# Issuing the adjacency strips of a graph kernel from two engines' DMA queues

## The chip, the cores and the metric

One core of one Trainium2 chip runs the whole program. The metric is the device time of one execution in microseconds; the median of the runs shown is what counts. A profiled execution gives the rows below.

## The reference

Two graph layers over 4096 nodes with 256 features, and a 0/1 adjacency matrix `adj` of 4096 x 4096 in float32. Cut to what matters:

```python
deg = max((adj != 0).sum(-1), 1)
pooled = (dinv * (adj + I) * dinv) @ x + x             # dinv = rsqrt(deg)
x = layernorm(x + relu(pooled @ W0 + b0))              # first layer
# second layer: h = x @ W_sa ; scores_ij = h_i.a_left + h_j.a_right
e = where(adj != 0, exp(-leaky_relu(scores, 0.01)), 0)
x_a = (e / (e.sum(1) + 1e-5)) @ h                      # attention branch
x_b = adj @ (x @ W_gcnb) + b_gcnb                      # plain branch
x = layernorm(x + sigmoid(gate_a * x_a + gate_b * x_b))
```

The gates are sigmoids of `adj @ x` and `x` projected to one column each. The adjacency is read from HBM once as float32 (64 MB) and turned into one-byte codes; both layers multiply with the codes.

## The kernel before

**Layer one, TensorE.** The rows of the output are 32 tiles of 128 (`T`), four of them to a quarter (`PT`). `sum_rows` (L1372) multiplies the codes of one quarter with `y` = x W0, split into a high and a low half-precision part, over all 32 column blocks. The first quarter is interleaved with the making of `y` (`xt_step` L1340, `z_step` L1355). From tile 4 on, `sum_tile` puts between the four parts of a tile a transpose of an earlier tile's normalised rows (`t_step`, L1392) and a projection with the weights of layer two (`p_step`, L1407). Each of these waits for other engines: `t_step(n)` for VectorE's `normalize`, `p_step(n)` for VectorE's `x1t_lo(n)` (L954) and `h_lo(n-1)` (L941).

**The adjacency.** It comes in 128 strips (`NSTRIP`) of 512 KB: strip `s` holds two column blocks (`SJ`) of quarter `s // 16`. They go into a ring of six buffers (`RING`), each with a semaphore `strip_in` of its own. A cast turns a strip into codes: ScalarE (`cast`, L513) casts the odd strips and all of strips 26 to 31, VectorE (L796) the other even ones; `on_act(s)` says which. `casts_until(s)` gives how many casts each of the two has made once strip `s` is done. The codes live in three slots, one for each quarter.

**SyncE's queue.** One loop over `s` issues all strips in order (L344). From strip 6 on it waits first for the cast of strip `s - 6`, which frees the buffer, whichever engine makes it (L340 to L342). At eight places (`CODES_AT`: after strips 32, 43, 53, 69, 85, ...) the same queue sends one quarter's codes to HBM for layer two: two DMAs of 1 MB (L332). The weights are loaded behind strip 4.

**ScalarE's order**, written out by hand: in the first 60 us, a copy `xt_copy`, one or two `y_hi` and a cast per step or two; then `cast(7)`, `x1t_copy(0)`, `cast(2)`, `x1t_copy(1)`, `proj_copies(0)`, `cast(1)`, `x1t_copy(2)`, `proj_copies(1)`, `forms_hi(0)`, `cast(1)`, `x1t_copy(3)`, `proj_copies(2)`, `proj_copies(3)`, `cast(3)`; then for each tile `proj_copies(n-3)`, `x1t_copy(n-2)`, in every second tile `forms_hi`, and `cast(2)`. `x1t_copy` (L553) also issues a DMA of 128 KB (L555), `proj_copies` begins with a wait and a DMA of 136 KB (L562), copies the projection out of the accumulator (L568 to L582) and so releases VectorE's `h_lo`. **VectorE's order** per tile: `degree`, `h_lo`, `residual`, `x1t_lo`, `stats`, `forms_lo` in every second tile, one cast, `normalize`, one cast.

Layer two (from about 320 us) reads the codes back from HBM and has no strips.

Of the kernel before, what the change touches and what calls it, by code (L numbers as in the profile page):

```python
# [19 lines left out]
PW = 256  # L20
# [3 lines left out]
SJ = 2  # L24
GS = T // SJ
NSTRIP = NQ * GS
RING = 6
# [65 lines left out]
def build(nc, x, adj, W0, b0, Wsa, asa, Wg, bg, Wa, ba, Wb, bb, out):  # L93
    def at(name, shape, dt, off):
        size = int(np.prod(shape[1:])) * mybir.dt.size(dt)
        assert off + size <= TOP, (name, off + size, TOP)
        return nc.alloc_sbuf_tensor_at(name, shape, dt, offset=BASE + off)
# [30 lines left out]
    strip = at("strip", [P, RING, SJ, 2 * PW], F32, O_S)  # L128
# [89 lines left out]
    with ExitStack() as ctx:  # L218
        ps = ctx.enter_context(nc.psum_tensor("ps", [P, 8, 512], F32))
        block_sem = lambda name: ctx.enter_context(nc.semaphore(name))  # L220
        S = {}
# [19 lines left out]
        x_in, strip_in = several("x_in", len(XCUT) - 1), several("strip_in", RING)  # L241
# [22 lines left out]
        adj_view = adj.rearrange("(j p) c -> p j c", p=P)  # L264


        on_act = lambda s: s % 2 == 1 or BOTH_AT <= s < 2 * GS

        def casts_until(s):

            mine = sum(on_act(i) for i in range(s + 1))
            return mine, s + 1 - mine

        def z_is_copied(eng, t):

            eng.wait_ge(*((S["zf_act"], t + 1) if t < ZACT else (S["zf_dve"], t + 1 - ZACT)))
# [34 lines left out]
        def _(sp):  # L311
            def load_weights():

                for half, c in ((H1, 0), (H2, P)):
                    sp.dma_start(wp[:, :, half], Wg[:, c:c + P].rearrange("(k p) d -> p k d", p=P)
                                 ).then_inc(S["wts_in"], 16)
                sp.dma_start(wp[:, :, WG:WC], Wsa.rearrange("(k p) d -> p k d", p=P)).then_inc(S["wts_in"], 16)
                for i, a in enumerate((Wa, Wb)):
                    sp.dma_start(wrow[4 * i:4 * i + 4, :], a.rearrange("o (r p) -> (o r) p", p=P)
                                 ).then_inc(S["wts_in"], 16)  # L320
                sp.dma_start(asab[:], asa.rearrange("o d -> (o d)").partition_broadcast(P)).then_inc(S["wts_in"], 16)
                sp.dma_start(b0b[:], b0.partition_broadcast(P)).then_inc(S["wts_in"], 16)
                sp.dma_start(bgb[:], bg.partition_broadcast(P)).then_inc(S["wts_in"], 16)
                sp.dma_start(sc[:, BAB.start:BAB.start + 1], ba.partition_broadcast(P)).then_inc(S["wts_in"], 16)
                sp.dma_start(sc[:, BAB.start + 1:BAB.stop], bb.partition_broadcast(P)).then_inc(S["wts_in"], 16)

            def codes_when_cast(qq):

                for sem, n in zip(("cast_act", "cast_dve"), casts_until(qq * GS + GS - 1)):
                    sp.wait_ge(S[sem], n)  # L330
                for h in range(2):
                    sp.dma_start(a8d[2 * qq + h], codes[:, qq % SLOTS, h]).then_inc(codes_out[qq % SLOTS], 16)  # L332
# [4 lines left out]
                sp.dma_start(xs[:, t0:t1, 0:D], x_view[:, t0:t1, :]).then_inc(x_in[c], 16)  # L337
            CODES_AT = [2 * GS, 2 * GS + GS // 2 + RING // 2] + [q * GS + GS + RING - 1 for q in range(2, NQ - 1)]
            for s in range(NSTRIP):
                if s >= RING:  # L340
                    sp.wait_ge(S["cast_act" if on_act(s - RING) else "cast_dve"],
                               casts_until(s - RING)[0 if on_act(s - RING) else 1])  # L342
                qq, g = s // GS, s % GS
                sp.dma_start(strip[:, s % RING], adj_view[:, g * SJ:(g + 1) * SJ, qq * 2 * PW:(qq + 1) * 2 * PW]  # L344
                             ).then_inc(strip_in[s % RING], 16)
                if s == WTS_AT:
                    load_weights()
                if s in CODES_AT:
                    codes_when_cast(CODES_AT.index(s))
# [66 lines left out]
        def _(pool):  # L416
# [15 lines left out]
            def z_with_bias(n):  # L432

                if n >= 2:
                    pool.wait_ge(S["r_ready"], n - 1)
                z_is_copied(pool, n)
                pool.tensor_tensor(zb[:, n % 2, :], zf[:, n, 0:D], b0b[:], ALU.add).then_inc(S["zb_ready"], 1)
# [44 lines left out]
        def cast_waits(eng, s):  # L482

            qq = s // GS
            eng.wait_ge(strip_in[s % RING], 16 * (s // RING + 1))
            if qq >= SLOTS:
                eng.wait_ge(S["acc_done"], PT * (qq - SLOTS + 1))
                eng.wait_ge(codes_out[qq % SLOTS], 32 * (qq // SLOTS))

        def codes_of(s):  # L490
            return codes[:, s // GS % SLOTS, :, s % GS * SJ:(s % GS + 1) * SJ, :].rearrange("p h j i -> p j h i")
# [14 lines left out]
        def _(act):  # L506
            todo = iter(ACT_CASTS)

            def cast(count):

                for s in [next(todo) for _ in range(count)]:
                    cast_waits(act, s)
                    act.activation(codes_of(s), strip_of(s), ACT.Copy, scale=float(EDGE - NONE),  # L513
                                   bias=float(NONE)).then_inc(S["cast_act"], 1)

            def xt_copy(t):

                act.wait_ge(S["xt_done"], t + 1)
                if t >= 2:
                    act.wait_ge(S["z_done"], t - 1)  # L520
                act.copy(xt[:, t % 2, :], XTP(t)).then_inc(S["xt_ready"], 1)
# [6 lines left out]
            def y_hi(t):  # L528

                z_is_copied(act, t)  # L530
                if t == 0:
                    act.wait_ge(S["sx_ready"], 1)
                act.activation(y[:, t, 0, 0:D], zf[:, t, 0:D], ACT.Copy, scale=sc[:, SX]).then_inc(S["yhi_ready"], 1)

            act.dma_start(w0[:], W0.rearrange("(k p) d -> p k d", p=P)).then_inc(S["w0_in"], 16)
            for t in range(T):
                xt_copy(t)
                if 1 <= t <= ZACT:
                    z_copy(t - 1)
                for i in split_at(t):  # L540
                    y_hi(i)
                if t in ACT_AT:
                    cast(1)
# [47 lines left out]


            cast(7)
            x1t_copy(0)
            cast(2)
            x1t_copy(1)
            proj_copies(0)
# [729 lines left out]
        def _(pe):  # L1327
# [15 lines left out]
            def z_step(t):  # L1343

                pe.wait_ge(S["xt_ready"], t + 1)
                if t == 0:
                    pe.wait_ge(S["w0_in"], 16)
                if t >= 2:
                    z_is_copied(pe, t - 2)
                if t == WT_AT:  # L1350
                    pe.wait_ge(S["wcol_ready"], 1)
                if t == WNORM_AT:
                    pe.wait_ge(S["wnorm_ready"], 1)
                for k in range(KD):
                    mm = pe.matmul(ZP(t), xt[:, t % 2, k * P:(k + 1) * P], w0[:, k, :], start=(k == 0),  # L1355
                                   stop=(k == KD - 1))
                mm.then_inc(S["z_done"], 1)
# [278 lines left out]
```

## Time and profile before

| | us |
|---|---|
| three runs | 876.67, 876.71, 878.2 |
| median | 876.71 |
| the profiled execution, its own time | 878.33 |
| span of its instructions | 876.2 |
| TensorE busy in the span | 855.4 (98%) |
| VectorE busy | 670.0 (76%) |
| ScalarE busy | 573.6 (65%) |
| strips: count, size, median from issue to landing | 128, 512 KB, 7.4 |
| codes to HBM: count, size, median to landing | 16, 1024 KB, 10.9 |

Engine names in rows: PE is TensorE (PEld its weight loads), ACT is ScalarE, DVE VectorE, POOL GpSimd, SP SyncE; a q behind a name is that engine's sequencer, which waits and issues DMAs. L344 is line 344 of the kernel. A matmul's end is modelled. The queue q1 carries SyncE's DMAs, q10 ScalarE's.

### The profile page before, as it was taken

The page shows a single profiled execution, that of the slowest core. Times are in us where ns is not written, and L with a number is a line of the kernel's source. Part 1 is how long each engine was busy: PE and PEld are TensorE (multiplying, and loading weights), DVE is VectorE, ACT ScalarE, POOL GpSimd, SP SyncE. Part 2 cuts the span into 40 slices and gives each one's busy share as a digit, 9 for nine tenths or more (in the row PEclk, how much of TensorE's full clock was granted, in tenths as well). Part 3 has the DMA queues.
Part 4 walks back from the last instruction along what each step waited for, and adds up shares of the span by engine and source line. Part 5 has one row for each costly group of instructions (what it writes and reads, how often), then busy time and mean ns, then how long its engine had stood idle before and what let it go on. Part 6 is the DMA issues. An engine that isn't in the chain of part 4 may idle for free.

```text
span 876.2 us, 20454 instructions
## 1 busy us (share of the span) xinstructions
PE 855.4 (98%) x7574; PEld 754.2 (86%) x7574; DVE 670.0 (76%) x1181; ACT 573.6 (65%) x1217; POOL 178.1 (20%) x181
## 2 busy tenths in 40 slices
PE   9999989999999998998899999999999999999997
PEld 7878778888888887887788888888888888888886
DVE  6686756665656468898988988988978978978863
ACT  5765545555555237988977876966966967867831
POOL 1013223222322221012022022032032032032021
PEclk9999999999999999999999999999999999999999
DMA  9889999999989433110220120120120120220001
GB/s 318 271 274 393 328 405 326 360 349 321 378 308 350 167 112 137 56 55 1 79 80 16 62 78 24 54 78 23 55 78 10 67 78 0 78 78 0 25 25 37
DMA packets 66649, 130.01 MB, mean 148 GB/s; under 512 B 5496, under 2 KB 29088, under 8 KB 62112
## 3 DMA queue, kind: packets, MB, share of 16 engines
q1 hardware_dynamic: 57392, 120.61, 38.8%
q10 hardware_dynamic: 9200, 8.64, 2.9%
q8 instruction: 36, 0.59, 0.3%
q14 instruction: 21, 0.17, 0.1%
HBM read 99.87 MB, written 29.36 MB: 147 GB/s over the span
## 4 chain that ended last, share of the span: by engine, by line
PE 81%; DVE 6%; ACT 4%; issue 4%; DMA 2%; POOL 1%; ACTq 0%; POOLq 0%; DVEq 0%; SPq 0%
PE ps L1535 30%; PE ps L1372 23%; PE ps L1476 19%; PE ps L1407 5%; PE ps L1355 3%; DMA strip<-in_adj_dram 2%; DVE ec L1106 2%; ACT ec L629 2%; DVE em L1113 1%; ACT em L638 1%; DVE dd L948 1%; PE ps L1392 1%; PE ps L1340 1%; PE ps L1331 0%; POOL sc L461 0%
## 5 line engine op out<-in xcount | busy, mean ns | idle before, releaser
L1535 PE MATMUL ps<-fb,em 128*128 128x257 f16 x3072 | 347.5, 273 | 0.8 <-DVE em L1113 0.8
L1535 PEld LDWEIGHTS ps<-fb,em 128*128 128x128 f16 x3072 | 300.4, 98 | 38.6 <-issue 1.3
L1372 PE MATMUL ps<-y,codes 128*128 128x257 f16 x2048 | 237.7, 273 | 0.7 <-DVE y L836 0.7
L1372 PEld LDWEIGHTS ps<-y,codes 128*128 128x128 fp8e4 x2048 | 200.4, 98 | 27.7 <-DVE y L836 1.1
L629 ACT ACTIVATE ec<-slb,nsb 128x256 f32<-128x256 f32 x512 | 211.1, 496 | 0.0
L1113 DVE SCALAR_TENSOR_TENSOR em<-ec,em 128x2048 f16<-128x2048 f32 x64 | 147.4, 2303 | 23.7 <-ACT em L638 23.7
L638 ACT ACTIVATE em<-ec 128x2048 f16<-128x2048 f32 x64 | 122.0, 1908 | 65.1 <-PE ps L1535 57.2
L1106 DVE SCALAR_TENSOR_TENSOR ec<-ec,pan 128x2048 f32<-128x2048 f32 x64 | 147.3, 2301 | 2.6 <-issue 1.8
L513 ACT ACTIVATE codes<-strip 128x1024 uint8<-128x1024 f32 x67 | 68.7, 1048 | 34.2 <-DMA strip<-in_adj_dram 33.2
L1476 PE MATMUL ps<-zz,dd 128*128 128x256 f16 x768 | 89.4, 273 | 1.5 <-DVE t L1135 1.3
L461 POOL TENSOR_TENSOR sc<-sc,sc 128x2 f32<-128x2 f32 x15 | 38.5, 2567 | 245.4 <-DVE sc L1215 245.4
L1476 PEld LDWEIGHTS ps<-zz,dd 128*128 128x128 fp8e4 x768 | 75.0, 98 | 10.6 <-issue 2.0
L455 POOL TENSOR_TENSOR w<-w,bgb 128x512 f32<-128x512 f32 x16 | 27.7, 1731 | 184.9 <-DVE w L1173 184.9
L948 DVE SCALAR_TENSOR_TENSOR dd<-pan 128x512 uint32<-128x512 uint32 (+2 forms) x85 | 64.1, 814 | 0.0
L1476 PE MATMUL ps<-fa,pan 128*128 128x260 f16 x512 | 60.0, 274 | 3.4 <-DVE s L1144 2.1
L1476 PE MATMUL ps<-fa,dd 128*128 128x260 f16 x512 | 59.6, 274 | 1.6 <-DVE m L1125 1.5
L1476 PEld LDWEIGHTS ps<-fa,pan 128*128 128x128 fp8e4 x512 | 49.9, 98 | 10.8 <-issue 2.3
L1476 PEld LDWEIGHTS ps<-fa,dd 128*128 128x128 fp8e4 x512 | 49.8, 98 | 9.0 <-issue 2.3
L964 DVE TENSOR_SCALAR lnst<-ps 128x1 f32<-128x1 f32 x32 | 5.0, 156 | 61.7 <-PE ps L1372 61.7
L1407 PE MATMUL ps<-wps,x1t 128*128 128x256 f16 (+1 forms) x384 | 49.0, 278 | 2.9 <-DVE x1t L954 2.9
L674 ACT ACTIVATE ot<-sg,sc 128x256 f32<-128x256 f32 x30 | 16.4, 593 | 52.4 <-POOL sc L465 52.4
L553 ACT ACTIVATE x1t<-ps 128x256 f16<-128x256 f32 x32 | 12.2, 381 | 56.0 <-PE ps L1392 56.0
(154 smaller groups left out, 789.0 us busy)
## 6 DMA issues: line engine op xcount, KB each, us to landing
strip<-in_adj_dram SPq DMA_DIRECT2D x128, 512.0 KB, 7.4
a_scratch<-codes SPq DMA_DIRECT2D x16, 1024.0 KB, 10.9
pan<-a_scratch SPq DMA_DIRECT2D x16, 1024.0 KB, 4.8
x_scratch<-x ACTq DMA_DIRECT2D x32, 128.0 KB, 5.2
x1r<-x_scratch SPq DMA_DIRECT2D x16, 256.0 KB, 2.7
h_scratch<-hst ACTq DMA_DIRECT2D x30, 136.0 KB, 4.8
out_dram<-ot SPq DMA_DIRECT2D x15, 256.0 KB, 2.2
fb<-h_scratch SPq DMA_DIRECT2D x3, 1088.0 KB, 8.7
```

Source lines behind the costliest of these rows:

```text
L455: pool.tensor_tensor(w[:], w[:], bgb[:].unsqueeze(1).broadcast_to([P, 2, D]), ALU.add).then_inc(S["bias_ready"], 1)
L461: pool.tensor_tensor(sc1[:, RS2], sc1[:, VE2], sc[:, MH2], ALU.pow).then_inc(S["yrstd_ready"], 1)
L513: act.activation(codes_of(s), strip_of(s), ACT.Copy, scale=float(EDGE - NONE), bias=float(NONE)).then_inc(S["cast_act"], 1)
L629: e_ = act.activation(ec[:, c % ER, jj, :], slb[:, slot, :], ACT.Exp, scale=-(1 - SLOPE), bias=nsb[:, jb:jb + 1])
L638: act.activation(em[:, c, 0], ec[:, c % ER], ACT.Copy, scale=MU / EDGE_VAL).then_inc(S["ehigh_ready"], 1)
L948: return dve.scalar_tensor_tensor(out=o, in0=b, scalar=0x7f7f7f7f, in1=a, op0=ALU.bitwise_and, op1=ALU.bitwise_xor)
L1106: dve.scalar_tensor_tensor(out=ec[:, c % ER], in0=ec[:, c % ER], scalar=1.0, in1=pan[:, slot, c * CH:(c + 1) * CH, :].bitcast(F8), op0=ALU ...
L1113: dve.scalar_tensor_tensor(out=em[:, c, 1], in0=ec[:, c % ER], scalar=MU / EDGE_VAL, in1=em[:, c, 0], op0=ALU.mult, op1=ALU.subtract).then ...
L1372: mm = pe.matmul(ACC(n), codes[:, qq % SLOTS, h, jb, e * P:(e + 1) * P].bitcast(F8), y[:, jb, part, 0:YC], start=(jb == 0 and part == 0), ...
L1407: mm = pe.matmul(b, x1t[:, n % 2, x_part, k * P:(k + 1) * P], wps[:, k, w_part, c0:c1], start=(k == 0 and x_part + w_part == 0), stop=(k = ...
L1476: mm = pe.matmul(ps[:, bank, 0:2 * c], a.bitcast(F8), g, start=(p == 0), stop=(p == NP - 1))
L1535: mm = pe.matmul(PH(2 * m + e)[:, 0:HC], em[:, c, e_part, i, e * P:(e + 1) * P], fb[:, jb, h_part, 0:HC], start=(jb == 0 and e_part + h_pa ...
```

## The change

The issue of a strip becomes a helper. SyncE keeps strips 0 to 5 and those whose buffer VectorE's cast frees. Behind each of its own casts of strip `s`, ScalarE waits for that cast to be complete and issues strip `s + 6`. As strips 26 to 31 are all ScalarE's, it issues the six strips 32 to 37 in a row; in all it issues 64 of the 128. The places in SyncE's loop at which codes are sent stay at the same `s`, whoever issues that strip.

```diff
+        def load_strip(eng, s):
+
+            qq, g = s // GS, s % GS
+            eng.dma_start(strip[:, s % RING], adj_view[:, g * SJ:(g + 1) * SJ, qq * 2 * PW:(qq + 1) * 2 * PW]
+                          ).then_inc(strip_in[s % RING], 16)
+
             for s in range(NSTRIP):
-                if s >= RING:
-                    sp.wait_ge(S["cast_act" if on_act(s - RING) else "cast_dve"],
-                               casts_until(s - RING)[0 if on_act(s - RING) else 1])
-                qq, g = s // GS, s % GS
-                sp.dma_start(strip[:, s % RING], adj_view[:, g * SJ:(g + 1) * SJ, qq * 2 * PW:(qq + 1) * 2 * PW]
-                             ).then_inc(strip_in[s % RING], 16)
+                if s < RING:
+                    load_strip(sp, s)
+                elif not on_act(s - RING):
+                    sp.wait_ge(S["cast_dve"], casts_until(s - RING)[1])
+                    load_strip(sp, s)
                 if s == WTS_AT:
                     load_weights()
                 if s in CODES_AT:
                     codes_when_cast(CODES_AT.index(s))
@@ ScalarE, cast(count)
                     cast_waits(act, s)
                     act.activation(codes_of(s), strip_of(s), ACT.Copy, scale=float(EDGE - NONE),
                                    bias=float(NONE)).then_inc(S["cast_act"], 1)
+                    if s + RING < NSTRIP:
+                        act.wait_ge(S["cast_act"], casts_until(s)[0])
+                        load_strip(act, s + RING)
```

## Rows read from the trace of the kernel before

**Rows 1.** Stretches: us; busy PE, PEld, DVE, ACT, POOL; TensorE clock, DMA share, GB/s.

```profile
60.00:90.00 30.00, 30.00 (x274) 26.53 (x273) 20.65 (x56) 17.28 (x36) 6.73 (x11) 1.00 1.01 375
...
102.00:116.00 14.00, 13.44 (x123) 11.76 (x121) 6.58 (x20) 5.08 (x11) 1.27 (x2) 1.00 1.04 409
...
120.00:124.00 4.00, 3.81 (x21) 2.81 (x22) 3.47 (x10) 3.17 (x8) 0.71 (x2) 0.58 1.08 428
136.00:320.00 184.00, 184.00 (x1674) 163.84 (x1673) 112.80 (x332) 86.21 (x216) 49.93 (x74) 1.00 0.83 298
```

**Rows 2.** Timeline of TensorE: start, us, work [idle before it <- what ended that].

```profile
21.27 1.13 PE L1355 MATMUL ps<-w,xt 128*128 128x256 f32 x4 [0.22 <-ACT xt L521]
...
95.79 0.44 PE L1392 MATMUL ps<-ident,x 128*128 128x128 f32 x2 [1.19 <-DVE x L998]
...
109.11 1.50 PE L1407 MATMUL ps<-wps,x1t 128*128 128x262 f16 x12 [0.56 <-DVE x1t L954]
...
120.19 2.77 PE L1407 MATMUL ps<-wps,x1t 128*128 128x262 f16 x12 [2.32 <-DVE x1t L954]
```

**Rows 3.** The chain that ended last, near 103 to 120 us: start, us, what.

```profile
102.96 12.59 DMA strip<-in_adj_dram
...
117.87 0.13 ACT hst L582
```

**Rows 4.** Who waited for whom up to 330 us: total us, times, longest.

```profile
ACT codes L513 <- DMA strip<-in_adj_dram: 33.2, 16, 5.5
...
DVE codes L796 <- DMA strip<-in_adj_dram: 7.1, 5, 1.9
```

**Rows 5.** The same for SyncE's queue.

```profile
SPq L344 <- DVE codes L796: 158.3, 45, 8.7
...
SPq L344 <- ACT codes L513: 23.6, 18, 4.1
```

**Rows 6.** Timeline of SyncE's queue, 88 to 120 us.

```profile
97.66 1.32 SPq L332 DMA_DIRECT2D a_scratch<-codes  x2
99.03 17.99 SPq L344 DMA_DIRECT2D strip<-in_adj_dram  x10
```

**Rows 7.** Strips 44 and 45: issue min/median/max ns, starts; issue to landing.

```profile
L344 SPq DMA_DIRECT2D strip<-in_adj_dram x2: 636/890/1143, 99.0 to 99.7; - x2
...
DMA to landing us min/median/max: 12.6/12.9/13.2
```

**Rows 8.** Strip 43, the same view.

```profile
L344 SPq DMA_DIRECT2D strip<-in_adj_dram x1: 522/522/522, 97.0 to 97.0; - x1
...
DMA to landing us min/median/max: 7.7/7.7/7.7
```

**Rows 9.** Strip 48, and all strips: issue times.

```profile
L344 SPq DMA_DIRECT2D strip<-in_adj_dram x1: 2704/2704/2704, 104.2 to 104.2; - x1
...
L344 SPq DMA_DIRECT2D strip<-in_adj_dram x128: 367/466/2704, 9.8 to 276.8; - x128
```

**Rows 10.** Timeline of ScalarE and its queue, 83 to 97 us.

```profile
83.34 0.44 ACTq L562 DMA_DIRECT2D h_scratch<-hst  x1
83.83 0.35 ACT L568 ACTIVATE q<-ps,sc 128x1 f32<-128x1 f32 x1 [0.49 <-issue]
...
87.86 1.04 ACT L513 ACTIVATE codes<-strip 128x1024 uint8<-128x1024 f32 x1
88.04 0.34 ACTq L555 DMA_DIRECT2D x_scratch<-x  x1
88.41 0.45 ACTq L562 DMA_DIRECT2D h_scratch<-hst  x1
...
89.07 0.34 ACT L568 ACTIVATE q<-ps,sc 128x1 f32<-128x1 f32 x1
```

**Rows 11.** Timeline of ScalarE later: the wait behind the casts of a tile.

```profile
94.25 2.94 ACT L513 ACTIVATE codes<-strip 128x1024 uint8<-128x1024 f32 x3
...
191.94 0.35 ACT L568 ACTIVATE q<-ps,sc 128x1 f32<-128x1 f32 x1 [1.42 <-PE ps L1407]
```

## What the change should do: the prediction

> **What bounds the kernel now.** Read TensorE's timeline first, for where it stands still. Up to 320 us it waits for ScalarE's or VectorE's results for 0.22 us at 21, 1.19 at 95, 0.56 at 109 and 2.32 at 118 to 120 [rows 2]; two more waits in the first 58 us (0.35 and 0.69) are for VectorE's own order and aren't touched by strips. From 136 to 320 us it is busy 184.00 of 184.00 us [rows 1]. So the change can win only in the four waits, 4.3 us, and in what follows the last: just behind it the granted clock is 0.58 over 120 to 124 us, that is, at the lower of its levels (1.2 GHz) for most of this stretch, and twelve matmuls take 2.77 us in place of 1.50 [rows 1, 2]. With the 0.30 us that the next ones lose, the low clock costs about 1.6 us here.
>
> The waits view tells who is held up by strips: ScalarE for 33.2 us in 16 waits, VectorE for 7.1 us in 5, TensorE itself practically never [rows 4]. The chain shows how a strip then reaches TensorE: strip 47 needs 12.59 us, its cast is in front of `proj_copies(5)` in ScalarE's order, the last copy of that ends at 118.00, and only then come VectorE's `h_lo(5)`, `residual(7)` and `x1t_lo(6)`, for which TensorE's `p_step(6)` starts at 120.19 instead of 117.87 [rows 2, 3].
>
> SyncE's queue shows what the change attacks. It waits 158.3 us for VectorE's casts, 23.6 us for ScalarE's [rows 5]: a strip whose buffer ScalarE has freed often stands behind one that VectorE has not. Strip 45 is the clearest: the three casts 35, 37, 39 end at 94.25 + 2.94 = 97.19 us, and 45 is issued at 99.7, behind two code writes of 1 MB issued from 97.66 [rows 6, 7, 11]. It lands 13.2 us after its issue. Strip 43, ahead of these writes, takes 7.7 us [rows 8].
>
> But the DMA engines are full at just that time: share 1.01 from 60 to 90 us, 1.04 (409 GB/s, so 1.28 us for a strip of 0.524 MB) from 102 to 116 [rows 1]. An earlier issue then changes the order in which strips come, not their number.
>
> **What the change does, step by step.**
>
> *ScalarE's own time.* Each of the 64 issues adds a wait for the cast's end and a DMA issue. ScalarE's queue needs 0.34 to 0.45 us for a smaller DMA, and the next instruction starts 0.05 us after it [rows 10]; on SyncE a strip's issue takes 0.47 us in the median, 0.37 at the least [rows 9]. Casts back to back now start 0.95 us apart though one takes 1.05 (three in 2.94 us) [rows 11]; that overlap of 0.1 us is lost too. I take 0.6 us for a cast, between 0.5 and 1.2 (the slowest issue beside much traffic was 1.14 us at strip 45, and 2.70 at 48, where SyncE's queue held four strips and the code writes; ScalarE's will hold three strips at most, so I leave the 2.70 to a rival) [rows 7, 9]. There is a second cost: the sequencer now runs ahead of the engine, and DMAs L555 and L562 are issued while a cast still runs (88.04 and 88.41 under the cast of 87.86) [rows 10]. Behind a wait for the cast they lose that cover: 0.34 + 0.45 us, of which the 0.36 us copy hides the first.
>
> *Steady state, 136 to 320 us.* For a tile ScalarE gets 2 x 0.6 + 0.33 = 1.5 us more. Behind its two casts it now waits 1.42 us for the projection in the tighter tiles [rows 11]. It will be 0.1 us late, and TensorE wants the result one tile, 8.6 us, later. Cost nothing; if strips were late besides (a wait of 2.6 us has been harmless there), still nothing, as those waits shorten. The cover is gone only beyond about 4 us of delay.
>
> *Stage one, 20 to 58 us.* At 21 us ScalarE is full and TensorE already waits for it [rows 2]. The next copy comes 0.6 us later, against some 0.45 us of room: 0.15 us lost. The later casts have an iteration of 2 us of room: nothing. Bounds 0 and 0.6.
>
> *The start of the tiles, 86 to 96 us.* Here ScalarE's order is the chain: cast 33 at 87.86, then `x1t_copy(3)`, `proj_copies(2)` with L568 at 89.07 [rows 10]. With the issue it is: cast to 88.90, issue to 89.40, copy and the two DMAs to 90.20, L568 at 90.25. That is 1.2 us later, and VectorE, which takes `h_lo(2)` next and then its cast and tile 5, hands it on to `normalize(4)`, for which TensorE waits at 95.79 [rows 2]. I add 1.2 us (bounds 0.6, if both DMAs still hide, and 1.7).
>
> *At 109 us.* TensorE arrives 1.2 us later. Strip 43 is issued by ScalarE, which is itself 0.9 us later but spared the wait behind 42. From then on the two queues share the engines, and 43 competes with the 2 MB of codes. I take it to land at about 105 instead of 104.7, its cast, issue and exposed DMA to put `proj_copies(4)` 1.2 us later, and the wait to stay as it is: 0.
>
> *At 120 us.* Strips 45 and 47 no longer stand behind the code writes in one queue; at half a share of the engines they land at about 110 and 112 instead of 112.9 and 115.6. ScalarE's last copy then ends near 116 rather than 118.00. What is late next is VectorE: strips 44 and 46 stay behind the writes and now share with 45, 47 and 49, so 46 lands at about 114.5, and with cast, `degree`, `h_lo`, `residual` `x1t_lo(6)` is through at 118 to 119. TensorE, by then shifted to 117.87 + 1.35 = 119.2, hardly waits: the 2.32 us wait goes, -2.2 us. This is the term that I know least: 0 if the shares go against ScalarE, -2.3 at best.
>
> *SyncE* loses 64 waits and issues and nothing is late by it; the code writes of the first quarter go out some 3 us earlier, at 67, where nobody waits for what they delay.
>
> The sum: 0.15 + 1.2 + 0 - 2.2 = about -0.9 us. In the profiled execution's own time 878.33 - 0.9 = 877.4, or 875.8 if the low clock (1.6 us) also goes with the wait that stood before it. The median 876.71 is 1.6 us below the profiled execution and one run was 878.2; I read that as two kinds of execution, with and without the low clock, and take the median to be one without. So 876.71 - 0.9 = **875.8 us**.
>
> The Trainium skill speaks against the change: DMA: Bandwidth & Descriptors, "Issuing engines are not separate DMA queues", says that transfers started by several engines run on the same 16 DMA engines and only the sequencer's issue time is saved. The trace agrees with the first half (full engines at 60 to 120 us, rows 1); it says nothing on the waits of an in-order queue, which are what is removed here. By that page alone the result would be the second rival's.
>
> **The rivals.**
> 1. *Bigger win*: strips of ScalarE overtake the code writes fully, the two DMAs stay hidden. Then the waits at 109 and 120 us go (2.9 us) against 0.15 + 0.3 us: -2.4, and with a low clock that the median did contain, -4.0: 874.3 to 872.7. For it: strip 45 loses 2.5 us before its issue and 5.5 us of ScalarE's time. Against: the full engines. Chance 0.25.
> 2. *Nothing comes of it*: the engines are full, the strips of one queue come earlier and those of the other later by as much, VectorE waits in place of ScalarE, and what ScalarE's issues cost in front of 95.79 is taken up by the wait at 120. 876.7, between 876.2 and 877.5. Chance 0.22. The change would in this case do what it says without effect.
> 3. *Slower*: the code writes win the sharing. If queues take turns by packets, one of 8 KB (codes) against one of 2 KB (strips), strip 43 gets a fifth of the bandwidth while 2 MB go out and lands at 107.8, 3.1 us late. TensorE then waits at 109 us 2.3 us longer, on top of 1.35, and reaches `p_step(6)` at 121.5: +1.3, and with the low clock of such a wait, now in every run, +2.9: 879.6. It decides if strip 43 lands after about 106. An issue of 2.7 us on ScalarE at 95 to 100 would act alike. Chance 0.14. (The Trainium skill, DMA: Bandwidth & Descriptors, "Queues, rings and completion order", says that each engine takes turns between its queues packet by packet; no row before shows two long queues at once.)
> 4. My forecast, between 875.0 and 876.4: chance 0.39.
>
> **How the numbers follow.** A measurement of this kernel can tell about 0.2%, 1.75 us, from no change: faster means below 874.96, slower above 878.46. The forecast and rival 2 are "same" (0.61, less 0.02 for their edges); faster 0.26, slower 0.15. The range: rival 1 reaches 872.7, rival 3 879.6; leaving out a tenth at either side gives 873.6 to 878.8.
>
> **What the profile after would show.** ScalarE's waits for strips fall from 33.2 us to under 20, VectorE's rise from 7.1 to over 10. L568 after cast 33 starts 1.2 us later than 89.07 and TensorE's wait at 95 grows by about that. The wait of 2.32 us at 120 falls below 0.5. Strip 43's landing separates forecast and rival 3; the order 45, 44, 47, 46 separates it from rival 2. From 136 us on TensorE stays full, shifted by a constant. I would be wrong if ScalarE's issue cost over 1 us, if the clock falls elsewhere, or if TensorE waited after 136 us.

## The result, and the profile after

| | before | after |
|---|---|---|
| median of 7 runs each (us) | 878.50 (876.67 to 880.22) | 884.10 (882.03 to 886.03) |
| ratio, 95% interval | 1 | 1.0062, 1.0044 to 1.0081 |
| profiled execution, its span (us) | 878.33, 876.2 | 884.1, 882.0 |
| TensorE busy, 60 to 136 us | 71.89 | 67.97 |
| TensorE busy, 136 to 320 us [rows 1] | 184.00 | 184.00 |
| median us to landing: strips | 7.4 (all SyncE's) | 7.8 (SyncE's), 8.0 (ScalarE's) |
| median us to landing: L563, L570 | 5.2, 4.8 | 6.5, 8.2 |

The change makes the kernel 0.62% slower (the medians differ by 5.6 us), where 875.8 us and a range of 873.6 to 878.8 were forecast. The three runs shown before the prediction sat low: with four more of the same kernel the median is 1.8 us higher. The ratio doesn't hang on that. Lines of the kernel after are those of before plus 5 to 8: the cast L518 (was L513), ScalarE's two small DMAs L563 and L570 (L555, L562), the projection's copy L576 (L568), `sum_rows` L1380 (L1372), `t_step` L1400 (L1392), `p_step` L1415 (L1407). A strip is issued at L277.

The stretches of after: us; busy PE, PEld, DVE, ACT, POOL; clock, DMA share, GB/s.

```profile
60.00:136.00 76.00, 67.97 (x585) 57.76 (x583) 47.85 (x132) 38.31 (x81) 17.53 (x27) 0.96 0.94 347
...
90.00:96.00 6.00, 4.98 (x46) 4.23 (x45) 3.42 (x10) 3.69 (x11) 0.00 (x0) 1.00 0.49 134
...
116.30:121.70 5.40, 5.39 (x26) 3.78 (x27) 2.34 (x6) 1.88 (x5) 0.55 (x1) 0.50 1.06 401
136.00:320.00 184.00, 184.00 (x1674) 163.84 (x1672) 110.71 (x326) 90.24 (x223) 51.04 (x75) 1.00 0.86 306
```

In this execution all is lost before 136 us; behind it TensorE is as full as before. Between 90 and 96 us the DMA engines, whose share was 0.88 there in before, now have 0.49: strips are missing because their casts, which free the buffers, are late. TensorE's timeline names the waits (the rows that stand against [rows 2]).

```profile
21.25 1.13 PE L1363 MATMUL ps<-w,xt 128*128 128x256 f32 x4 [0.75 <-ACT xt L529]
...
73.63 0.44 PE L1400 MATMUL ps<-ident,x 128*128 128x128 f32 x2 [0.86 <-DVE x L1006]
79.20 0.44 PE L1400 MATMUL ps<-ident,x 128*128 128x128 f32 x2 [0.28 <-DVE x L1006]
83.73 0.61 PE L1380 MATMUL ps<-y,codes 128*128 128x257 f16 x4 [1.01 <-ACT codes L518]
95.50 1.49 PE L1415 MATMUL ps<-wps,x1t 128*128 128x262 f16 x12 [1.02 <-issue]
100.07 0.44 PE L1400 MATMUL ps<-ident,x 128*128 128x128 f32 x2 [1.32 <-DVE x L1006]
...
116.31 2.77 PE L1415 MATMUL ps<-wps,x1t 128*128 128x262 f16 x12 [3.49 <-DVE x1t L962]
118.88 5.07 PE L1380 MATMUL ps<-y,codes 128*128 128x257 f16 x32
...
124.00 3.68 PE L1380 MATMUL ps<-y,codes 128*128 128x257 f16 x32
```

Against before: 2.15 us of new waits at 73, 79 and 83; 2.34 instead of 1.19 at 95 and 100; 0.56 less at 109; 3.49 instead of 2.32 at 116. That is +3.9 us, and by the windows TensorE's busy time falls by 71.89 - 67.97 = 3.9. The clock adds 1.1: at 0.50 twelve matmuls take 2.77 instead of 1.50 us and 32 take 5.07 instead of the 3.68 of the next tile, 2.7 us in all against 1.6 before. The wait at 21 us has 0.5 us more, of which more below. Together 5.5 of the span's 5.8 us.

ScalarE and its queue in after (the same view as [rows 10]):

```profile
71.96 1.06 ACT L518 ACTIVATE codes<-strip 128x1024 uint8<-128x1024 f32 x1 [4.36 <-DMA strip<-in_adj_dram]
73.04 0.37 ACTq L277 DMA_DIRECT2D strip<-in_adj_dram  x1
73.47 1.06 ACT L518 ACTIVATE codes<-strip 128x1024 uint8<-128x1024 f32 x1 [0.45 <-ACT codes L518]
74.55 0.38 ACTq L277 DMA_DIRECT2D strip<-in_adj_dram  x1
74.97 1.06 ACT L518 ACTIVATE codes<-strip 128x1024 uint8<-128x1024 f32 x1 [0.45 <-DMA strip<-in_adj_dram]
...
80.10 1.05 ACTq L563 DMA_DIRECT2D x_scratch<-x  x1
81.26 0.35 ACT L576 ACTIVATE q<-ps,sc 128x1 f32<-128x1 f32 x1 [0.80 <-issue]
...
82.62 1.05 ACT L518 ACTIVATE codes<-strip 128x1024 uint8<-128x1024 f32 x1
...
90.83 1.04 ACT L518 ACTIVATE codes<-strip 128x1024 uint8<-128x1024 f32 x1
...
92.39 0.38 ACT L561 ACTIVATE x1t<-ps 128x256 f16<-128x256 f32 x1 [0.52 <-ACT codes L518]
92.42 0.39 ACTq L563 DMA_DIRECT2D x_scratch<-x  x1
...
93.34 0.35 ACT L576 ACTIVATE q<-ps,sc 128x1 f32<-128x1 f32 x1 [0.57 <-issue]
...
99.91 1.06 ACT L518 ACTIVATE codes<-strip 128x1024 uint8<-128x1024 f32 x1 [0.47 <-ACT codes L518]
100.99 0.40 ACTq L277 DMA_DIRECT2D strip<-in_adj_dram  x1
101.44 1.06 ACT L518 ACTIVATE codes<-strip 128x1024 uint8<-128x1024 f32 x1 [0.48 <-ACT codes L518]
102.53 0.38 ACTq L277 DMA_DIRECT2D strip<-in_adj_dram  x1
...
103.03 1.51 ACTq L563 DMA_DIRECT2D x_scratch<-x  x1
104.59 0.42 ACT L595 ACTIVATE fa<-gb 128x260 f16<-128x260 f32 x1 [1.20 <-issue]
```

Three things are to be seen. An issue leaves ScalarE idle for 0.45 to 0.52 us, and casts in a row start 1.5 us apart instead of 0.95 [rows 11]. The small DMA behind the cast no longer runs under it. And the small DMA's own issue takes 1.05 us at 80.10 and 1.51 at 103.03 instead of 0.34, with five and three strips under way in ScalarE's queue and the engine idle behind it (at 92.42, with one, it takes 0.39). The cast at 82.62 (strip 31, which closes the quarter) is the one that TensorE waits for at 83.73; before, it began at 79.66.

VectorE shows a fourth, on strip 24, which stays with SyncE. In before it was issued at 62.0 us and landed 3.9 us later:

```profile
65.98 0.69 DVE L796 TENSOR_SCALAR codes<-strip 128x1024 uint8<-128x1024 f32 x1 [1.57 <-DMA strip<-in_adj_dram]
```

In after it was issued at 62.3 us, with strip 25 already on its way in ScalarE's queue since 61.3 and strip 27 following there at 62.8, and needed 7.0 us:

```profile
69.28 0.69 DVE L804 TENSOR_SCALAR codes<-strip 128x1024 uint8<-128x1024 f32 x1 [4.27 <-DMA strip<-in_adj_dram]
...
73.17 0.41 DVE L1006 TENSOR_SCALAR x<-x,lnst 128x256 f32<-128x256 f32 x1 [0.67 <-POOL lnst L451]
```

VectorE casts it in front of the work on the first tile, so the `normalize` (L1006) that TensorE waits for at 73.63 is late by the same 3.3 us (69.86 in before). Strip 26, issued at 62.9, lands at 71.9, so that ScalarE's cast 26 starts at 71.96 instead of 69.28.

### The profile page after: what moved, and what is told of

Its sections match the earlier page's. It is cut to its first block, busy times and chain, and to the rows that moved or that the text cites. A ratio compares the mean times of both kernels' runs of the same rounds, so it can differ in the third digit from the quotient of the medians.

```text
span 882.0 us, 20454 instructions
## 1 busy us (share of the span) xinstructions
PE 856.7 (97%) x7574; PEld 754.2 (86%) x7574; DVE 670.0 (76%) x1181; ACT 576.6 (65%) x1217; POOL 178.2 (20%) x181
## 4 chain that ended last, share of the span: by engine, by line
PE 78%; DVE 7%; ACT 5%; issue 4%; DMA 4%; ACTq 1%; SPq 0%; POOL 0%; POOLq 0%; DVEq 0%
PE ps L1543 30%; PE ps L1380 22%; PE ps L1484 19%; PE ps L1415 5%; DMA strip<-in_adj_dram 2%; DVE ec L1114 2%; ACT ec L637 2%; PE ps L1363 2%; DMA xs<-in_x_dram 1%; DVE em L1121 1%; ACT em L646 1%; ACT codes L518 1%; DVE dd L956 1%; PE ps L1400 1%; DVE sc L811 1%
## 5 line engine op out<-in xcount | busy, mean ns | idle before, releaser
L1380 PE MATMUL ps<-y,codes 128*128 128x257 f16 x2048 | 238.9, 274 | 1.6 <-ACT codes L518 1.0
L1380 PEld LDWEIGHTS ps<-y,codes 128*128 128x128 fp8e4 x2048 | 200.9, 98 | 29.3 <-ACT codes L518 1.3
L518 ACT ACTIVATE codes<-strip 128x1024 uint8<-128x1024 f32 x67 | 70.4, 1052 | 33.7 <-DMA strip<-in_adj_dram 21.8
L1484 PEld LDWEIGHTS ps<-fa,pan 128*128 128x128 fp8e4 x512 | 49.9, 98 | 10.8 <-issue 2.3
L1415 PE MATMUL ps<-wps,x1t 128*128 128x256 f16 (+1 forms) x384 | 49.0, 278 | 4.6 <-DVE x1t L962 3.5
L804 DVE TENSOR_SCALAR codes<-strip 128x1024 uint8<-128x1024 f32 x61 | 42.5, 700 | 9.3 <-DMA strip<-in_adj_dram 9.3
## 6 DMA issues: line engine op xcount, KB each, us to landing
a_scratch<-codes SPq DMA_DIRECT2D x16, 1024.0 KB, 10.8
```

The costliest lines, as they stand in the source:

```text
L804: dve.tensor_scalar(codes_of(s), strip_of(s), float(EDGE - NONE), float(NONE), ALU.mult, ALU.add).then_inc(S["cast_dve"], 1)
L1380: mm = pe.matmul(ACC(n), codes[:, qq % SLOTS, h, jb, e * P:(e + 1) * P].bitcast(F8), y[:, jb, part, 0:YC], start=(jb == 0 and part == 0), ...
L1415: mm = pe.matmul(b, x1t[:, n % 2, x_part, k * P:(k + 1) * P], wps[:, k, w_part, c0:c1], start=(k == 0 and x_part + w_part == 0), stop=(k = ...
L1484: mm = pe.matmul(ps[:, bank, 0:2 * c], a.bitcast(F8), g, start=(p == 0), stop=(p == NP - 1))
```

## The experiments

Two theories. **Theory S**: the loss is ScalarE's own time, the wait for its cast, the issue, and what stands behind them in its order. **Theory Q**: it is the sharing between the two queues, above all strips beside the code writes, whose packets are four times as large. Every ratio is against runs of the kernel before on the same chip, made together with it.

**The parts of S, with all strips issued by SyncE as before.** `wait_only` adds the wait alone; `small_dma` puts a DMA of 32 KB behind it, `tiny_dma` one of 8 KB, from a constant to a scratch tensor that nothing reads (the diff is that of `tiny_dma`; `small_dma` has `ident[:, 0:64]`, `wait_only` the wait alone, behind every cast). None of the three takes a strip's issue from SyncE. `small_dma` adds 2 MB in all and `tiny_dma` 0.5 MB to the 64 MB of strips.

```diff
                                    bias=float(NONE)).then_inc(S["cast_act"], 1)
+                    if s + RING < NSTRIP:
+                        act.wait_ge(S["cast_act"], casts_until(s)[0])
+                        act.dma_start(tinyd[s], ident[0:16, 0:128]).then_inc(S["tiny_out"], 16)
```

> The kernel before, with one thing of the change: ScalarE waits for the end of each of its own casts. SyncE issues all strips. Theory S (the loss is ScalarE's own time: waits, issues, lost cover of its other DMAs): about 0.1 us for each cast plus the DMAs L555 and L562 out of cover behind the cast of strip 33, so 0.5 to 1.2 us slower, with the wait at 95 us grown by about 0.8. Theory Q (the loss is that two queues take turns and strips land out of the order of their use): 0 to 0.5 us, no wait of TensorE at 73 to 84 us.

Measured: 879.61 us, 1.0009 (0.9995 to 1.0022).

> The kernel before, but ScalarE waits for the end of each own cast and then issues a DMA of 32 KB into a scratch in DRAM, 64 of them; all strips stay in SyncE's queue. So ScalarE pays nearly the whole time of the change while the strips keep their order. Theory S: 4 to 6 us slower, as the change itself (5.6), with waits at 73 to 84 us and one of 3 us or more near 116. Theory Q: 1 to 2.5 us slower, from the first cast and from the chain behind the cast of strip 33; nothing at 73 to 84 us, strip 24 lands near 66 and strip 43 7 to 8 us after its issue.

Measured: 882.36 us, 1.0040 (1.0026 to 1.0053).

> As small_dma, but each of ScalarE's 64 DMAs is 16 rows of 512 bytes (8 KB), so it costs ScalarE its wait and issue and loads the DMA engines with almost nothing; all strips in SyncE's queue. Theory S (ScalarE's time): still 3 to 5 us slower than before. If small_dma was slow by its traffic, under 1.5 us. The waits at 83 (cast of strip 31) and 94 us stay in theory S.

Measured: 883.55 us, 1.0056 (1.0037 to 1.0075). TensorE's timeline of `tiny_dma`:

```profile
82.76 0.61 PE L1377 MATMUL ps<-y,codes 128*128 128x257 f16 x4 [1.02 <-ACT codes L515]
94.43 1.49 PE L1412 MATMUL ps<-wps,x1t 128*128 128x262 f16 x12 [0.91 <-issue]
98.99 0.44 PE L1397 MATMUL ps<-ident,x 128*128 128x128 f32 x2 [1.32 <-DVE x L1003]
114.06 1.50 PE L1412 MATMUL ps<-wps,x1t 128*128 128x262 f16 x12 [2.31 <-DVE x1t L959]
125.56 1.84 PE L1412 MATMUL ps<-wps,x1t 128*128 128x262 f16 x12 [2.75 <-DVE x1t L959]
```

and its window (columns as above):

```profile
60.00:136.00 76.00, 67.65 (x592) 58.10 (x591) 48.78 (x135) 38.38 (x81) 17.43 (x27) 0.98 0.97 357
```

A DMA that carries almost nothing costs about as much as the change: the waits at 83, 95 and 100 us are the same to about 0.1 us, and busy time is 67.65 against 67.97. The wait for the own cast alone is hardly measurable; the issue behind it is what costs. The rest isn't the same. The waits of after at 73 and 79 us, 1.14 us in all, are missing (strip 24 is cast at 66.66 here); and where after waits 3.49 us at 116 with the low clock behind it, `tiny_dma` waits 2.31 at 114 and 2.75 at 125.

**The change on its own, and the DMA, again on one chip.**

> The changed kernel again, unaltered, to stand beside the next one on the same chip. 5 to 6 us slower than before by every theory.

Measured: 883.83 us, 1.0057 (1.0039 to 1.0075). Between 73 and 116 us it has the waits of after, to 0.4 us each; besides, 1.51 us at 22 and 0.89 us at 145.78.

> The kernel before with ScalarE's waits and 64 small DMAs, strips all in SyncE's queue, again, beside the changed kernel. If ScalarE's time is about two thirds of the loss and the sharing of the engines by two queues of strips the rest, it is 3 to 4 us slower than before and 1.5 to 2.5 us faster than the changed kernel. If sharing costs nothing, both are the same; if sharing is all, this is the same as before.

Measured: 882.98 us, 1.0054 (1.0035 to 1.0074). On the same chip the two can't be told apart. The ratios leave 0.03% to Theory Q and the medians 0.10%, but by the intervals it can be up to about 0.3%; the first `small_dma`, at 1.0040, was further from the change.

**Where.** ScalarE issues only a part of its strips, SyncE the rest. The diff against after is that of `act_to31`; the others have 32 <= s < 54, s >= 54, 32 <= s < 38 and s = 39 in its first line:

```diff
+        by_act = lambda s: RING <= s < 2 * GS and on_act(s - RING)
-                elif not on_act(s - RING):
-                    sp.wait_ge(S["cast_dve"], casts_until(s - RING)[1])
+                elif not by_act(s):
+                    mine = 0 if on_act(s - RING) else 1
+                    sp.wait_ge(S[("cast_act", "cast_dve")[mine]], casts_until(s - RING)[mine])
                     load_strip(sp, s)
-                    if s + RING < NSTRIP:
+                    if by_act(s + RING):
```

> The change for strips up to 31 only: ScalarE issues strips 7 to 31 whose buffers its casts free, SyncE the rest in order. Theory Q: strip 24 lands near 69 and not 66, TensorE waits at 73, 79 and 84 us for about 2 us in all, and about 2 us stay to the end as no later wait is for less than that: 1.5 to 3 us slower. Theory S: the casts of the run of seven cost 0.5 us each, but most are waits for strips before, so under 1 us slower.

Measured: 879.61 us, 1.0016 (1.0003 to 1.0028). Strip 24 is cast at 68.33, and TensorE waits 0.42 us at 72.68, but not at 79 or 83. So Theory Q had the strip and one of its three places right; the loss of 1.4 us (0.3 to 2.5) decides nothing between its 1.5 to 3 us and Theory S's under 1 us. The wait at 73 us is there in every kernel in which ScalarE issues strips 25 to 31 right behind its casts, and in none in which SyncE issues them: it comes from the second queue.

> The change for strips 32 to 53 only. Both theories: nothing up to 84 us. Then Theory Q: strip 43 shares the engines with the code writes, lands 9 us or more after its issue, and TensorE's wait for it grows to 2.5 us or more: 2 to 4 us slower. Theory S: the chain behind the cast of strip 33 costs 1.2 us, the later wait only what the exposed DMAs cost, 1 to 2 us slower.

Measured: 882.11 us, 1.0041 (1.0027 to 1.0054).

> The change for strips 54 to 127 only, where TensorE never waits: 37 of the 64 issues. Both theories: no change within 0.1%, as two more ScalarE issues for a tile fit into its waits and a strip has several us in hand. If it is slower by 0.1% or more, the steady part pays too.

Measured: 878.39 us, 1.0000 (0.9987 to 1.0012). The three parts add up to 0.57% of 0.62. The steady stretch, 37 of the 64 issues, costs nothing that can be measured. Most comes from 32 to 53, 14 issues; two kernels look into them (strips 41 to 53 were not tried alone):

> The change for strips 32 to 37 only: six issues behind the casts of strips 26 to 31. Theory S: the cast of strip 31 is late, TensorE waits about 0.9 us at 82 us, all later shifted by it, but the waits behind 95 us end with strips whose issue SyncE makes later too: 0.5 to 1.5 us slower at the end. Theory Q: the first code writes share the engines with these strips, nothing that TensorE waits for: 0.

Measured: 880.05 us, 1.0013 (1.0003 to 1.0024); TensorE waits 0.31 us at 78 and 0.59 at 82, and 2.31 at 121 as before.

> The change for one strip, 39: ScalarE issues it behind the cast of strip 33, SyncE all others in order. Theory S: p_step(3) waits 1.0 us at 92 and the wait at 96 stays, so 1.1 us of shift; strip 41 and the code writes follow it, so 0.5 to 1.2 us slower in the end. Otherwise no change.

Measured: 880.32 us, 1.0017 (1.0007 to 1.0027). A single issue out of 128 costs 1.5 us (0.6 to 2.4): the one behind cast 33. TensorE's timeline of `act_39only`:

```profile
92.47 1.49 PE L1418 MATMUL ps<-wps,x1t 128*128 128x262 f16 x12 [1.03 <-issue]
97.03 0.44 PE L1403 MATMUL ps<-ident,x 128*128 128x128 f32 x2 [1.31 <-DVE x L1009]
110.81 1.50 PE L1418 MATMUL ps<-wps,x1t 128*128 128x262 f16 x12 [1.02 <-DVE x1t L965]
123.25 2.77 PE L1418 MATMUL ps<-wps,x1t 128*128 128x262 f16 x12 [3.68 <-DVE x1t L965]
```

It shows the pair of waits at 92 and 97 us, 2.34 instead of 1.19, exactly as in after. And the later waits don't shrink by it, they grow (1.02 for 0.56, 3.68 for 2.32). How much is open, as this execution, 881.24 us, was the slowest of eleven.

**The remedy that S suggests**: ScalarE issues the strip behind its next instruction, so that it needn't stand still for its own cast. `issue_owed` makes the wait and the issue; it stands behind the next cast, and behind `xt_copy`, `x1t_copy` and L576.

```diff
+                    issue_owed()
                     if s + RING < NSTRIP:
-                        act.wait_ge(S["cast_act"], casts_until(s)[0])
-                        load_strip(act, s + RING)
+                        owed.append(s)
```

> The changed kernel, but ScalarE issues a strip only behind its next instruction (the next cast, copy or projection copy), so that the wait for its own cast and the issue lie under that instruction; who issues which strip stays as in the change. If the loss is ScalarE's time (theory S), most of it comes back: within 0.15% of the kernel before, waits of TensorE at 84 and 95 us gone. If it is the sharing of the engines by two queues (theory Q), it stays 0.4% or more slower, with the waits at 73 and 116 us.

Measured: 881.23 us, 1.0037 (1.0024 to 1.0051): 0.25 of the 0.62% come back, where Theory S had expected most of it. The wait at 83 us is now 1.82:

```profile
82.93 0.61 PE L1391 MATMUL ps<-y,codes 128*128 128x257 f16 x4 [1.82 <-ACT codes L526]
```

The small DMA (L573 here) is issued at 78.49 behind ScalarE's own strips, and its issue takes 1.86 us; ScalarE stands for 2.00 us, the copies (L586 first) follow, and cast 31 comes behind them, at 81.83 (strip 31 had landed at 80.32). The waits view (total us, times, longest) has this wait:

```profile
ACT q L586 <- issue: 4.3, 3, 2.0
```

Covering the wait for the cast isn't enough; the issues themselves still take the sequencer.

**The rival Q.** First its sign in after, from the DMA engines between 108 and 111 us (queue: packets, MB, share):

```profile
q1 hardware_dynamic: 140, 1.01, 79.9%
q10 hardware_dynamic: 141, 0.27, 23.0%
```

With code writes in SyncE's queue q1 and strips in ScalarE's q10 the two get equally many packets, 140 and 141, and SyncE's move 3.7 times the bytes. The Trainium skill (DMA: Bandwidth & Descriptors, "Queues, rings and completion order") has each engine take turns between queue rows packet by packet; the equal counts agree. So the third rival's mechanism is real. Two runs take it away from strip 43: `after_codes_later` sends the second quarter's codes after strip 49 instead of 43 (`CODES_AT = [2 * GS, 49] + ...`), `after_codes_2k` stores the codes in rows of 2 KB instead of 8, so that packets are alike. `codes_later` is the former for the kernel before.

> The changed kernel with the code writes of the second quarter after strip 49 in place of 43. Theory Q: strip 43 no longer shares the engines with them, lands about 5 us after its issue and not 9.8, and the wait of 3.5 us at 116 us goes: 2 to 4 us faster than the changed kernel, still 2 us slower than before by the waits up to 100 us. Theory S: the wait shrinks by less than 1.5 us.

Measured: 884.73 us, 1.0071 (1.0057 to 1.0085). Strip 43 lands 7.9 us after its issue instead of 9.8, about as quickly as before [rows 8]. TensorE's wait behind it is 1.59 us instead of 3.49, but 1.23 us at 136 and 1.40 at 146 are there instead.

> The changed kernel with the codes in DRAM laid out so that a code write's rows are 2 KB as the strips' are, not 8 KB; the same bytes. If the queues take turns packet by packet, strip 43 now gets half of the bandwidth beside the writes and not a fifth, lands 7 to 8 us after its issue, and TensorE's wait at 116 us shrinks by 1.5 to 2.5 us. If they share by bytes or time, nothing changes there.

Measured: 885.18 us, 1.0071 (1.0053 to 1.0088). Strip 43 needs 9.0 us, but now the code writes take 13 to 17 us and a strip behind them 18.6. TensorE waits 2.67 us at 115 instead of 3.49 at 116, less of a gain than expected, and 1.87 at 122. (Layer two also reads the codes back in rows of 2 KB here, so the total time isn't that of the writes alone.)

> The kernel before with one size changed: the code writes of the second quarter go out after strip 49 and not after strip 43; SyncE issues everything. Strips 44 to 47 then need no longer stand behind 2 MB of writes and land some 4 to 5 us earlier, and the wait of 2.3 us at 120 us should go: 1 to 3.5 us faster. If this wait has another cause, no change.

Measured: 878.27 us, 1.0003 (0.9992 to 1.0015). The wait of 2.32 us at 120 is gone, and one of 1.89 us at 138 is there.

None gains: Q's mechanism is there, but taking it away at this place doesn't bring the time back. `codes_later` shows besides what my sum had missed: in this stretch, where the engines are full, a wait for strips that is taken away returns a few tiles later.

**Is it the order, or the supply?** Cast 33 stands in front of the chain that ends at 95 us. `swapped` makes it (and VectorE's cast 32) before the work for layer two:

```diff
-            forms_hi(0)
             cast(1)
+            forms_hi(0)
             x1t_copy(3)
```

> The kernel before with SyncE issuing all strips, and one swap on each engine at 85 to 90 us: the cast of strip 33 goes in front of forms_hi(0) on ScalarE, the cast of strip 32 in front of forms_lo(0) on VectorE, both under a wait that stands there now (1.51 and 1.06 us). Strips 38 and 39 are then issued 2 us earlier, while the DMA engines run dry, and x1t_copy(3) follows 1 us earlier. If the order of ScalarE's and VectorE's work at that place sets TensorE's later waits and not the queue, the waits at 95, 109 and 120 us shrink by 1.5 to 3 us in all: 1 to 3 us faster. If not, no change.

Measured: 877.67 us, 0.9999 (0.9984 to 1.0013); no wait at 109, but 3.16 us at 120. Again the wait has only moved. So the next step is to take the code writes out of the full stretch. `spread` changes one line of the kernel before (`CODES_AT` has seven entries, not eight; the last quarter's codes go out behind the loop), `swapped_spread` has both edits, `after_swapped_spread` both on top of the change:

```diff
-            CODES_AT = [2 * GS, 2 * GS + GS // 2 + RING // 2] + [q * GS + GS + RING - 1 for q in range(2, NQ - 1)]
+            CODES_AT = [2 * GS, 55, 67, 79, 91, 104, 117]
```

> The kernel before with SyncE issuing all strips, the two swaps of swapped, and the code writes of quarters two to six at later places (after strips 55, 67, 79, 91, 104 in place of 43, 53, 69, 85, 101), out of the stretch where the DMA engines are full. If the supply of strips there sets TensorE's waits at 109, 120 and 138 us, these go and only the one at 95 stays: 1.5 to 4 us faster than before. If not, no change.

Measured: 873.90 us, 0.9946 (0.9932 to 0.9960).

> Kernel before with the code writes spread (strips 32, 55, 67, 79, 91, 104, 117) and the order of the casts 33 and 32 as it was. swapped alone gave 0.9999 and swapped_spread 0.9946. If the supply of strips between 99 and 140 us sets the waits behind 109 us, the spread alone takes most of it: 0.9955 to 0.9965, 873.9 to 874.8 us, with TensorE's waits of 1.19 us at 95 us kept and at most 0.6 us at 109. If both edits are needed (a strip-bound wait is only moved, as with codes_later), it stays within 0.9985 to 1.0010.

Measured: 874.14 us, 0.9956 (0.9940 to 0.9972).

> The changed kernel with the two edits of swapped_spread (the two casts 33 and 32 ahead of forms_hi(0) and forms_lo(0); code writes spread to strips 32, 55, 67, 79, 91, 104, 117). Theory S (ScalarE's own time for each issue ends as TensorE's waits at 83, 95 and 100 us, where no later strip-bound wait can take it up): the loss against swapped_spread is at least the 0.57% of the change, since its time of 873.9 has only the wait at 95 us left in it; I expect 877.5 to 879 us, ratio 1.001 to 1.003. Rival (the loss comes mostly from strips 41 to 47 beside the code writes, and the stretch of 102 to 124 us): with the writes moved out of that stretch the change costs 0.1 to 0.2%, 875 to 876 us, ratio 0.998 to 0.999.

Measured: 877.86 us, 0.9994 (0.9981 to 1.0007). The window of `swapped_spread`:

```profile
60.00:136.00 76.00, 74.90 (x679) 66.01 (x678) 53.84 (x149) 42.86 (x93) 21.11 (x32) 1.00 0.99 360
```

The window of `spread`:

```profile
60.00:136.00 76.00, 74.77 (x678) 65.90 (x676) 54.37 (x150) 42.37 (x93) 21.14 (x32) 1.00 0.99 357
```

The window of `after_swapped_spread`:

```profile
60.00:136.00 76.00, 71.97 (x644) 62.30 (x642) 51.40 (x143) 41.39 (x90) 20.27 (x31) 1.00 0.95 337
```

Spreading the writes is worth 0.44% by itself: of before's four waits only those at 21 and 95 us are left, and up to 136 us the clock stays at 1.00. It is the version to keep. With it, ScalarE's issues cost 0.43% (877.86 against 874.14 on one chip, the latter without the swap) or 0.48% (0.9994 / 0.9946), in TensorE's waits of 0.54, 0.16, 0.31 and 0.88 us between 73 and 84, and 0.95 at 113. I had expected 1.001 to 1.003 if S were all and 0.998 to 0.999 if Q were most; it lies between. So of 0.62% some 0.4 to 0.5 stay when the full stretch of 102 to 124 us and its low clock are gone, and 0.1 to 0.2 need that stretch. The 0.4 to 0.5 aren't all Theory S's: the wait at 73 us, 0.54, comes from strip 24 beside ScalarE's queue, cast at 69.64 here too, and the first quarter's codes are still written from 70.8 us on. What ScalarE's waits and issues cost without any of it is `small_dma` and `tiny_dma`, 0.40 to 0.56%. They are the larger part, then; what the sharing of the queues adds in the end, these runs can't say more exactly.

## Why the prediction was wrong, point by point

- **A cast costs 0.6 us more: right.** Idle 0.45 to 0.52 behind each issue, and 1.5 us from cast to cast instead of 0.95.
- **First casts, +0.15.** The wait at 21 us is 0.75 instead of 0.22, but 0.79 in `act_32to37`, 0.46 in `act_39only` and 1.59 in `codes_later`, where nothing before 60 us is changed. Not to be told from the scatter of the input loads.
- **The stretch of 60 to 84 us: not in the sum. The first failed step, 2.15 us of waits, 1.01 of them at 83.** I had costed the queue's issue where "casts have an iteration of 2 us of room" and went on to 86 us. Between lie `cast(7)`, `cast(2)` and `cast(1)`, ten casts with ten issues, and TensorE needs the last one's codes for the next quarter. [rows 1] showed TensorE full up to 90 us, and I took full to mean slack behind it. Cast 31 comes 3.0 us later, for two reasons: cast 26 already starts 2.7 us later, as strip 26 lands late, and from there on the casts are up to 1.5 us apart even when their strips are there. Without any late strip the casts' issues are enough for a wait of about this size: `tiny_dma` has 1.02 us, `small_dma` 0.90 and `act_32to37` 0.59.
- **"ScalarE's will hold three strips at most": wrong.** At 80.10 us it held five (32 to 36), and three were enough: L563's issue took 1.05 us there, 1.51 at 103.03 with three, and 3.29 in `act_32to53` at 101.47, again with three. I had left this price, 2.70 us in [rows 9], to a rival; it belonged to the forecast wherever L563 stands behind casts in a row.
- **"Nothing is late by it" (SyncE): wrong.** SyncE's strips 24 and 26 were issued on time and landed late beside ScalarE's, 7.0 us after the issue instead of 3.9 for strip 24: the wait at 73 us, 0.86 us. The wait of 0.28 at 79 stays open (`act_32to37` has 0.31 there with strip 24 on time, `act_to31` none with it late). The first code writes went out at 70.48 us instead of 70.84, not at 67.
- **Start of the tiles, +1.2: right.** L576 starts 2.51 us behind cast 33's start instead of 1.21, so 1.30 later, and the two waits that follow have 1.15 more. `act_39only` has this term alone, and 1.5 us at the end.
- **109 us, 0: wrong by way of the strips.** Strip 43 was to land at about 105. The three casts began at 98.39 instead of 94.25, their distance had grown, and so ScalarE issued 43 at 100.99 instead of 97.0 [rows 8] and 45 at 102.53 instead of 99.7: later, though no longer behind the code writes. The chain of waits in after (start us, us, what):

```profile
98.50 0.95 ACT codes L518
...
99.91 1.07 ACT codes L518
...
100.99 9.83 DMA strip<-in_adj_dram
...
110.85 1.07 ACT codes L518
...
112.35 0.50 ACTq L570
...
116.31 2.77 PE ps L1415 x12
```

- **120 us, -2.2: wrong, and the largest failure.** It was to be the gain. The order in which strips landed was as forecast, 45, 44, 47, 46, but at 115.4, 117.5, 119.0 and 120.2 us instead of about 110 to 114.5. TensorE waited 3.49 us, at 116. I had set the delay of the chain at 95 against strips that come at a fixed time. But the strips' issues, and the code writes, stand behind the same late casts, and the delay moves them too; what wasn't transferred between 90 and 96 us, at the share of 0.49, is missing behind it. (Nor were the engines full all the way from 60 to 120 us before, as I wrote: 0.88 between 90 and 96.) `act_39only` has both in one run, 2.34 us and 3.68 us.
- **Steady stretch, 0: right as far as can be measured.** `act_from54` 1.0000; 184.00 us busy in both profiles. "If TensorE waited after 136 us" was named as a sign of being wrong, and `after_again` has one such wait, 0.89 us at 145.78, the tail of the stretch before; none later.
- **ScalarE's wait for strips** fell from 33.2 [rows 4] to 21.8 us in 12 waits (under 20 was forecast), VectorE's rose from 7.1 to 9.3 (over 10). Gained where it cost nothing. The waits of after up to 330 us (total us, times, longest):

```profile
ACT codes L518 <- DMA strip<-in_adj_dram: 21.8, 12, 4.4
...
ACT codes L518 <- ACT codes L518: 10.7, 20, 0.8
DVE codes L804 <- DMA strip<-in_adj_dram: 9.3, 8, 4.3
```

- **The base of the forecast, 876.71: low by 1.8 us.** I read three runs as two kinds of execution, with and without the low clock, and took the median to be one without. Of 101 later runs of the kernel before, 31 have a mean granted clock of 0.999 and a median of 877.05 us; the other 70 have 0.992 to 0.998, and those at 0.997, the most frequent, 878.57. So there is something in the two kinds, but the usual execution has the lower mean clock.
- **The third rival** had the right sign and symptoms: strip 43 9.8 us in flight, TensorE waiting longer, the low clock behind it; 879.6 was its time. Its cause was the lesser one, since `tiny_dma` has nearly the same loss without two queues of strips. Its last sentence, on an issue of 2.7 us on ScalarE, was the nearer one.
- **The Trainium skill** (DMA: Bandwidth & Descriptors, "Issuing engines are not separate DMA queues") says that issuing from several engines saves only the sequencer's time. The runs agree in that the second queue brought no bandwidth (347 GB/s against 372 over 60 to 136 us in before), and show the reverse side: no run shows a gain from SyncE's time, and it was paid for with ScalarE's, 0.5 us a strip.

## What to carry to other kernels

Before moving a DMA's issue to a computing engine, add for every place in that engine's written order, not only for the ones at which another engine already waits, the wait for its own result, the issue, and the DMAs behind it that used to be issued under the running instruction; and count how many transfers its queue then holds. Ask also which transfer of the other queue now has to share: strip 24 was issued on time and still came 3.3 us late. In this kernel, while the DMA engines were full, a wait for data that was removed at one place returned a little later, and a delay of the consumer also delayed the transfers that its buffers free: don't set the one off against the other. What did help was to take other traffic (the code writes) out of the stretch in which the loads are the bound.

## What the runs showed of the hardware

- The issue of a DMA of 128 KB on ScalarE's queue takes 0.34 us in before, and 1.05, 1.51 and 3.29 us with three to five strips of 512 KB ahead of it (1.86 in `after_deferred`), but 0.50 in `act_32to37` with five. The strips' own issues stayed at 0.37 to 0.46 us in after, and in `tiny_dma`, with DMAs of 8 KB ahead of it, it took 0.69, 0.88 and 1.28 us. So it isn't the bytes in the queue alone; what sets it stays open.
- A DMA of 8 KB holds ScalarE for as long as one of 512 KB: idle 0.39 to 0.47 us against 0.45 to 0.52.
- Beside strips in the other queue, a strip issued at the same time in the kernel took 7.0 us to land instead of 3.9 (strip 24).
- Behind TensorE's waits of 2.32 (before), 3.49 (after) and 3.68 us (`act_39only`) the granted clock fell to 0.50 (1.2 GHz) and twelve matmuls took 2.77 us. Behind waits of 2.31 us in `tiny_dma` and 3.11 us in `small_dma` they took 1.50, so the length of a wait doesn't decide it alone.
- Writing the second quarter's codes in rows of 2 KB instead of 8 KB raised their flight from 10 to 13 us to 13 to 17 us beside the same strips; over all sixteen writes the median rose from 10.8 to 12.3 us.
